# Other chunk borders in the last routed stage of a two-layer vision tower on one core

## The reference, cut to what matters

```
combine = _route(xf, router_weight, router_bias)   # 4 of 16 experts per token, from 2 of 4 groups
out = jnp.zeros_like(xf)
for e in range(E):                                 # E = 16, H = 256, I = 128
    g = xf @ w_gate[e].T
    u = xf @ w_up[e].T
    y_e = jax.nn.silu(g) * u @ w_down[e].T
    out = out + combine[:, e:e + 1] * y_e
```

## Time and profile before

| | |
|---|---|
| median of 3 runs | 1568.02 us (1556.63, 1568.02, 1570.49) |
| profiled execution | 1556.42 us |
| its span, first to last instruction | 1554.6 us |
| busy, share of the span | PE 89%, PEld 78%, DVE 67%, ACT 49%, POOL 40% |
| mean granted clock of PE | 0.939 of full speed |
| the last layer in the span | from about 1159 us on |
| its parts | front to 1207.8, first dense pair to about 1256, sorted units to about 1494, second dense pair to about 1537, then the last combines |

### The profile page before, as it was taken

How to read it: one execution, slowest core, us unless ns; L and a number is a source line. 1 busy time by engine, 2 the same in 40 slices (tenths; PEclk the granted TensorE clock), 3 DMA queues, 4 the chain that set the end, 5 groups by cost and what they waited for, 6 DMA issues and landing times. The chain is left out here.

```text
span 1554.6 us, 36959 instructions
## 1 busy us (share of the span) xinstructions
PE 1381.6 (89%) x14188; PEld 1213.2 (78%) x14188; DVE 1043.1 (67%) x2204; ACT 765.5 (49%) x1297; POOL 624.4 (40%) x552
## 2 busy tenths in 40 slices
PE   6989999999999996668987898888976899999995
PEld 5877788888888886668987566666755899999994
DVE  4744664764854755876676478888867786667775
ACT  5423444444444443325554576777731346666641
POOL 4006321111021000536625265543346656672775
PEclk9999999999999998789999899999975899999997
DMA  8304665262362301425865000000017258897973
GB/s 293 122 16 160 211 202 163 72 201 92 111 201 87 106 2 54 187 75 180 246 193 171 7 29 28 29 22 1 3 51 288 101 166 256 266 289 250 291 216 110
DMA packets 142883, 215.56 MB, mean 139 GB/s; under 512 B 14337, under 2 KB 112769, under 8 KB 141825
## 3 DMA queue, kind: packets, MB, share of 16 engines
q1 hardware_dynamic: 122368, 160.40, 31.2%
q0 software_dynamic: 18624, 52.45, 10.7%
q10 hardware_dynamic: 1728, 0.41, 0.1%
HBM read 103.64 MB, written 109.58 MB: 137 GB/s over the span
## 5 line engine op out<-in xcount | busy, mean ns | idle before, releaser
L125 PE MATMUL e_p_gu<-e_w_hi,e_xt_hi 128*128 (+1 forms) x676 | 201.0, 297 | 8.2 <-DVE e_xt_lo L713 6.0
L125 PE MATMUL e_p_gu<-e_w_lo,e_xt_hi 128*128 (+1 forms) x676 | 194.9, 288 | 0.0
L125 PE MATMUL e_p_gu<-e_w_hi,e_xt_lo 128*128 (+1 forms) x676 | 194.9, 288 | 0.0
L125 PEld LDWEIGHTS e_p_gu<-e_w_hi,e_xt_hi 128*128 128x128 f32 x676 | 133.1, 197 | 10.1 <-issue 8.9
L1255 POOL DMA_INDIRECT e_xn<-results,e_row_of x112 | 114.9, 1026 | 61.3 <-issue 33.5
L125 PEld LDWEIGHTS e_p_gu<-e_w_lo,e_xt_hi 128*128 128x128 f32 x676 | 133.4, 197 | 0.1
L125 PEld LDWEIGHTS e_p_gu<-e_w_hi,e_xt_lo 128*128 128x128 f32 x676 | 133.2, 197 | 0.0
L125 PE MATMUL e_p_y<-e_w_hi,e_hid_hi 128*128 (+1 forms) x338 | 111.3, 329 | 7.3 <-DVE e_hid_lo L732 7.1
L1238 POOL DMA_INDIRECT rows<-e_xn,e_row_of x96 | 95.1, 991 | 55.3 <-issue 28.6
L1920 DVE TENSOR_TENSOR a_ot_lo<-a_O,a_ot_hi 128x1024 fp32r<-128x1024 f32 x32 | 39.1, 1223 | 115.2 <-ACT a_ot_hi L1863 115.2
L125 PE MATMUL a_J<-a_xt_hi,w_qk_hi 128*128 128x512 f32 x256 | 106.6, 416 | 8.2 <-DVE a_xt_lo L1938 6.1
(11 more groups left out here) (336 smaller groups left out, 4354.1 us busy)
## 6 DMA issues: line engine op xcount, KB each, us to landing
e_moved<-rows SPq DMA_DIRECT2D x121, 256.0 KB, 3.6
results<-e_y SPq DMA_DIRECT2D x121, 256.0 KB, 3.5
rows<-a_zero SPq DMA_DIRECT2D x28, 1024.0 KB, 5.8
pa_x<-in_x SPq DMA_DIRECT2D x7, 1536.0 KB, 6.3
w_qk_in<-in_we SPq DMA_DIRECT2D x24, 384.0 KB, 6.3
we_parts<-w_qk_in SPq DMA_DIRECT2D x24, 384.0 KB, 2.6
we_parts<-a_e_lo SPq DMA_DIRECT2D x24, 384.0 KB, 2.5
e_w_hi<-we_parts SPq DMA_DIRECT2D x4, 1536.0 KB, 16.2
```

Of the source, the lines that this page charges most:

```text
L125: mm = eng.matmul(out, lhs[a], rhs[b], start=start and n == 0, stop=stop and n == len(terms) - 1, skip_group_check=skip)
```

## The change

The chunks get 6, 10 and 12 blocks in place of 8, 12 and 8, and the dense blocks are 16 to 19 in place of 20 to 23. Nothing else is edited, so `MOVES` and the numbers of `combine1` stay.

```
-CHUNKS = ((0, 8), (8, 20), (24, 32))
-DENSE = (20, 24)
+CHUNKS = ((0, 6), (6, 16), (20, 32))
+DENSE = (16, 20)
```

## The result

The changed kernel takes 1605.62 us (median of 4 runs, 1604.99 to 1608.03) against 1562.33 us of the kernel before in the same comparison (4 runs, 1552.43 to 1570.49). The ratio is 1.0301, 95% interval 1.0266 to 1.0336: slower by 3.0%, about 47 us (0.0301 x 1562; the two medians alone differ by 43.3). The profiled execution took 1605.5 us with a span of 1603.7 us and a mean granted clock of 0.929.

A forecast was written before the change was run, and what follows sets the result against it. PE was taken to bound the sorted steps and POOL's in-order issues the end; -5.5 + 2.9 + 1.0 + 32.4 + 21.2 = +52 us gave 1608 on the profile, 1620 on the median, forecast 1615, range 1592 to 1636.

The forecast's parts named there:

- The middle wait: DVE waits ahead of chunk 0's first combine for gathered rows: 32.4 us, bounds 28 to 36.
- the tail: From chunk 2's first gather to the end: 48 POOL issues in place of 32, 21.2 us more, bounds 20.3 to 22.
- the head start of PE against its low clock: When DVE goes on after its wait: some 1.5 us gained by PE, 1.7 us lost to half clock, taken as cancelling.
- The front: Start of the last layer, up to the first dense hidden values: earlier, smaller first routing, -5.5 us, bounds -2.5 to -10.
- The routing of chunk 1 in the dense pair: Routing at 10 blocks, inside the dense pair: slightly shorter, counted as nothing.
- The moved own units: Two pairs moved among chunk 0's sorted units: 1.44 us each, +2.9 us for two, upper bound +7.5.
- the routing of chunk 2: Routing at 12 blocks inside sorted steps; the piece with the maxima overruns its step: +1.0 us, bounds 0 and 3.
- the level: Median before lay 11.6 us above the profiled execution; 1615 was taken between 1608 and 1620.
- rival 1: The middle wait repeats at the next five combines, 1 to 2 us each, +7 us: 1622; chance 0.08.
- rival 2: The middle wait doesn't come, rows are there by step 67: +20 us, 1576 on the profile, 1588 on the median; chance 0.09.
- Rival 3: Not slower: POOL issues get cheaper when DVE and sorted DMAs are quiet; at 0.75 us, 1564; chance 0.03.
- the prediction's estimate: By the skill's rule, POOL issues at 0.62 + 0.30 us in DVE's wait and after PE's end: saves about 17 us, 1598.

The follow-up runs named there:

- The three versions that move the combine or its chunk: The changed kernel, 1605.62 us; the changed kernel with chunks of 8, 8 and 12 blocks, 1602.89 us; the kernel before with chunk 0's combines 6 steps sooner, 1567.5 us.
- The half-byte version: The changed kernel with chunk 2's scatter and gather moving 128 of 256 columns per row, same number of issues: 1609.71 us, 1.0304 of before.
- the late combine: The changed kernel with the combines of chunk 0 set 12 steps later and those of chunk 1 set 5 steps later: 1584.55 us, 1.0172 of before.
- the short version: The changed kernel with those later combines and the last four blocks of chunk 2 neither gathered nor combined: 1556.98 us, 0.999 of before.

## Why the prediction was right, point by point

**The direction, and the two large terms.** 1605.6 us lies in the range and 9 us below the forecast. The middle wait was given as 32.4 us and is 32.15; the tail as 21.2 and is 73.0 - 51.5 = 21.5. The three versions that move the combine or its chunk (32.15, 20.69, 11.21 us against 32.4, 21.2 and 11.8 by the same sum, the second from 2 x 2.80 + 20.6 - 5.0) confirm the sum itself, steps times 2.80 plus issues times 1.29 less 5.0: it wasn't one lucky figure. The half-byte version confirms what it rests on, the issue.

**What the wait costs.** I put the whole wait into the path and set the head start of PE against its low clock. Measured between the first scatter and the first gather of chunk 2, the changed kernel has 1429 matmuls in 202.4 us:

```profile
1328.30:1530.70 202.40, 169.50 (x1429) 168.33 (x1428) 117.25 (x252) 107.12 (x235) 112.04 (x112) 0.92 0.73 231
```

The kernel before has 1483 there, two sorted steps more, in 175.1 us:

```profile
1328.00:1503.10 175.10, 174.68 (x1483) 173.11 (x1482) 123.97 (x270) 111.10 (x244) 113.91 (x112) 1.00 0.88 274
```

At its pace 1429 take 174.68 x 1429 / 1483 = 168.3 us. The changed kernel is busy for 169.5, 1.2 us more, and idle for 32.9, of which the one wait is 31.7. So by this account the wait is whole in the path, 34.1 us with the 1.2. Behind the wait the half clock can be read by itself, and then the full one:

```profile
1400.10:1404.00 3.90, 3.84 (x19) 3.81 (x20) 3.25 (x7) 0.96 (x2) 2.99 (x3) 0.53 0.35 105
1404.00:1410.00 6.00, 6.00 (x53) 6.00 (x53) 3.58 (x8) 3.67 (x9) 4.50 (x5) 1.00 0.79 237
```

At the pace of the second row the 19 matmuls of the first would take 2.15 us and not 3.84, an estimate of 1.7 us for the clock, which is what the prediction had. But the version with the late combine, the same work without the wait, takes more than 168.3 in its own such stretch:

```profile
1328.80:1502.70 173.90, 171.18 (x1429) 167.10 (x1428) 117.31 (x252) 107.29 (x235) 111.63 (x113) 1.00 0.85 269
```

It loses 5.6 us in small pieces, which the version with the wait doesn't have: PE is idle for 2.7 us and, at full clock throughout, busy for 2.9 us more than 168.3. Against it the wait is worth 202.4 - 173.9 = 28.5 us. In the short version the same stretch is 175.8 us long. That is why the short version came out above a plain subtraction, and a part of why the late combine did; the rest of it lies in runs without a trace. What the pieces are is settled in one place only, in the short version:

```profile
1394.80 0.66 PE L1576 MATMUL e_p_xt<-ident,e_moved 128*128 128x128 f32 x4 [2.29 <-DMA e_moved<-rows]
```

PE waits 2.29 us for rows that SP loads, the granted clock behind it is 0.55 to 0.60 until 1400, and that step takes 7.59 us in place of 2.80. These are 4.8 of its 7.5 us above 168.3.

**The front.** -5.96 us against -5.5. The earlier start of the routing was 2.5 us (15.14 to 12.64 us behind the marker), against 2.47, and from there the way to the first dense hidden values is 35.6 us in place of 39.1, 3.5 shorter against 3.0 of the working. Here are the start of the routing, at 96 columns (6 blocks of 16 experts) in place of 128, and the first dense hidden values, answering to the earlier trace rows:

```profile
1169.88 0.34 DVE L1377 TENSOR_TENSOR e_work<-e_scores,router_bias 128x96 f32<-128x96 f32 x1 [0.90 <-ACT e_scores L1318]
...
1205.51 0.60 DVE L1357 SCALAR_TENSOR_TENSOR e_gated<-e_gated,e_comb,e_p_gu 128x128 f32<-128x128 f32 x2
```

**A term left at nothing that wasn't.** The routing of chunk 1 in the dense pair was put at "slightly shorter: nothing". From the first dense to the first sorted hidden values it is 41.77 us in place of 44.62, 2.85 less, and every version with 10 blocks in that chunk repeats it (41.8 to 41.9), while the kernel before with only its combine moved has 44.5. With 8 blocks it is 41.5, so the step between 10 and 12 isn't one of so much per block. DVE's busy time fell by 1.7 us (33.48 to 31.75) and PE's idle time by 2.4 (5.5 to 3.1); which came first I didn't test.

**The moved own units and the routing of chunk 2.** Given as 2.9 + 1.0. From the first sorted hidden values to the first scatter of chunk 2 it is 81.06 us in place of 69.86, 11.2 more, of which two steps of 2.80 are the later `routed`: 5.6 remain against 3.9. This point (+1.7 us) takes back part of the last one (-2.85) and of the front (-0.5); that the sum comes out within 1 us is luck to that extent.

**The sum and the level.** The last layer is 51.15 us longer, the sum said 52. On the profiled execution that gave 1608; the measured one took 1605.5, and 2.05 us of the difference lie ahead of the layer (the marker at 1157.24 in place of 1159.29). The forecast of 1615 missed by the level: I added 7 us for the runs of before that lay higher than the profiled one. The changed kernel's own runs spread over 3 us only, next to the lower level.

**The rivals.** The wait didn't repeat: 0.18 us at the second combine, none at the next three (rival 1). It came, so rival 2 falls as stated, but the late combine shows what it would have been: 1.0172, where 20 us would be 1.0128, just outside its interval. In its trace the last layer is 21.0 us longer than before (416.3 against 395.3), close to the 20 of the rival; the difference lies in its other runs. Rival 3, cheaper issues while DVE is quiet, can be read in one place, POOL grouped by line over the 32 us of DVE's wait, and over the 36 us ahead of it, in which DVE is busy for 24 us:

```profile
L1238 POOL DMA_INDIRECT rows<-e_xn,e_row_of x20 | 19.5, 973 | 6.1 <-issue 6.1
```

```profile
L1238 POOL DMA_INDIRECT rows<-e_xn,e_row_of x29 | 28.4, 981 | 40.5 <-DVE e_row_of L1473 31.9 <-issue 8.5
```

973 ns with DVE standing still, 981 with DVE at work, and 0.30 us between them in both: the price of an issue didn't fall when DVE stopped. The Trainium skill, "SBUF — State Buffer", "A bandwidth-pool intuition that's wrong", has GpSimd's DMA descriptors held up by DVE operations in a two-port mode and gives 620 ns for a DMA alone. No POOL row here shows that figure or such a hold-up. No run shows whether any DVE operation here is in such a mode, and the prediction's estimate put the time of a whole DMA in place of POOL's 0.97 us per issue. That estimate had 1598, which is 8 us low.

**What the profile should show.** The one wait of about 32 us with PE idle beside it, the half clock behind it, the 48 scatters in a row, the first gather directly behind, and the 48 gathers from the last stored result on: all there. From PE's last product (1564.0) to the end are 39.7 us, against some 39. The first dense product came at 1197.05, which is 1199.1 with the later marker of before, 3 us ahead of the 1202 given; PE then waited 3.6 us for the first hidden values, so DVE's work, as assumed, set the front.

## What to carry to other kernels

Where a queue is strictly in order and each of its instructions has a fixed price, count the issues between the moment that frees them and the moment that needs their result, on both sides of a change: that sum gave three different waits to within 0.6 us. A smaller first piece that starts earlier also brings forward whatever is placed a fixed number of steps behind it; if its supply stands in the queue behind the larger last piece, both shifts add up into one wait. And the last piece should be judged by what stands behind its last result. Here the gathers already outlasted the dense units that cover them, so each added issue cost 1.33 us.

## What was not expected of the hardware

An indirect DMA of 128 rows cost POOL the same 61.5 us for 48 scatters whether a row carried 256 columns or 128, at 229 or 179 GB/s in the same stretch, and the same 0.97 + 0.30 us whether DVE worked or stood still for 32 us. And the longer wait didn't cost PE more in clock than the shorter one. The granted clock was 0.50 at the restart in both. After 32 us PE went on at 1400.16 and was back at 1.00 by 1404; after 11 us, in the kernel before with its combine moved, it went on at 1380.65 and was back by 1388:

```profile
1380.60:1388.00 7.40, 7.35 (x41) 7.38 (x42) 4.63 (x10) 2.79 (x6) 5.61 (x6) 0.62 0.61 167
1388.00:1390.00 2.00, 2.00 (x19) 2.00 (x19) 0.75 (x2) 1.26 (x4) 1.39 (x3) 1.00 0.76 224
```

At the pace of the second row the 41 matmuls of the first would take 4.3 us and not 7.35, an estimate of 3.0 us, against 1.7 behind the wait of 32 us.
